# Adjacency ring of a fused graph network: zeroing only the last columns of each slot

## The chip, the core and the metric

The kernel runs on one core of a Trainium2 chip. The metric is the device time of one execution in microseconds (us), the median of several runs. Its engines are named as in the profile: PE (matrix products) with PEld (its weight loads), DVE (VectorE), ACT (ScalarE), POOL (GpSimd), SP (the queue that issues most transfers).

## What is computed

Two graph layers over 3125 nodes with 128 features and 53125 edges (25000 random pairs in both directions and one loop per node), sorted by target node `dst`. Each layer is followed by a residual and a layer norm.

```python
def _L0_gnn_ref(h, src, dst, etype, norm, weight, w_comp, bias_param):
    hsrc = h[src]
    coef = w_comp[etype]
    msg = jnp.zeros((hsrc.shape[0], weight.shape[2]), dtype=h.dtype)
    for b in range(weight.shape[0]):                       # 8 bases
        msg = msg + hsrc @ weight[b] * coef[:, b][:, None]
    msg = msg * norm
    node_repr = jax.ops.segment_sum(msg, dst, num_segments=h.shape[0])
    return jax.nn.relu(node_repr + bias_param)

def _L1_gnn_ref(node_feat, edge_feat, src, dst, eps, W1, b1, gamma, beta, W2, b2):
    msg = node_feat[src] + edge_feat
    neigh = jax.ops.segment_sum(msg, dst, num_segments=node_feat.shape[0])
    rst = (1.0 + eps[0]) * node_feat + neigh
    h = rst @ W1 + b1
    h = (h - jnp.mean(h, 0)) * jax.lax.rsqrt(jnp.var(h, 0) + 1e-5) * gamma + beta
    return jax.nn.relu(h) @ W2 + b2

x = _layernorm(x + _L0_gnn_ref(x, src, dst, edge_type_32, edge_weight1, ...))
x = _layernorm(x + _L1_gnn_ref(x, edge_attr_128, src, dst, ...))
```

## The kernel before

**Tiles, units, pairs.** The 53125 edges are 416 tiles of 128. Two tiles are a *unit* (208 units, `U`), two units a *couple* (the step `w` of DVE), four units a group, eight units a *pair* of groups (26 pairs, `PAIRS`; `PU` = 8). Since edges are sorted by target, the targets of a unit lie within a window of 20 nodes (`WIN`), and those of a pair within 132 (`SPAN`).

**First layer.** For each tile POOL gathers the 128 source rows of `x` (L719) into a ring of 32 tiles. PE multiplies them with selection matrices that DVE builds (L1302, L1312), for the 8 bases (L1004) and for the edge features of the second layer (L1010), into PSUM. DVE adds the window to `sums` (L1514). When enough units are in, a chunk of 512 nodes goes through the bases (L1034), the residual and the norm (L1042, L1406 to L1423, L1049), with ACT for the relu, the deviation and a copy (L815, L821, L826).

**Second layer, by counts.** The sum over neighbours is taken as a product with an adjacency matrix of counts. For each unit DVE makes one-hot keys of the source nodes, six units ahead (`keys_hot`, L1390 and L1393). PE turns them into counts, 25 blocks of 128 source nodes (`HIGHS`) by 20 target columns (L1025), in one of three PSUM banks. ACT copies these into the slot of the pair in SBUF, `adj_ring`, which has two slots: 25 blocks of 144 columns (`SPREAD`), float16. Unit 0 of a pair is copied to columns 0 to 19 (L805). Each later unit begins in a column that the unit ahead may also have filled, so its first column goes aside (`side`, L807) and is added by DVE (`shared_column`, L1484), and its other 19 are copied over what is there (L809), to where a register says. After the 8 units SP stores the slot to HBM (`store_adjacency`, L569), as soon as DVE has added the last shared column. Later SP loads blocks of two pairs again (L601), PE multiplies them with the first layer's result (L1058, which reads columns 0 to 131), and DVE adds the windows (L1468).

**Zeroing.** Columns that no unit of a pair copies must be zero. Before, ACT zeroes the whole slot, 3600 elements per partition in 8 pieces of 450 (`zero_adjacency`, L783). For pair 0 this comes ahead of everything; for pair p+1 it comes in two pieces behind each of the copies of units 4 to 7 of pair p, and ahead of the first of them ACT waits (`adj_out`) until the store of pair p-1, which used the same slot, has landed. DVE, PE and SP don't know of the zeroing; ACT itself waits for it ahead of unit 0 of a pair (`adj_zeroed`).

**Order of the work.** Every engine runs one list written out at build time. PE does the sums of unit u, then the counts of one or two units (`counted`: five units of counts for four of sums, so counts run ahead), and at set steps bases, transposes or a run of L1058 products. Counts of unit u wait until unit u-3 is copied. The sums of a couple wait until DVE has added the couple three back. DVE does per couple: the windows, keys, a block of L1468, the shared columns of the units that PE has counted some steps ahead, parts of the norm, and selection matrices. ACT copies in order of units, with L815, L821 and L826 between.

**The checks.** Whether all this holds for the input (windows, spans) is found early on one partition: DVE writes how far each limit is exceeded into `excess`, takes the maximum (L1347) and sets a flag (L1348). If it is above 0, all engines take a general and much slower path (`wide`).

## Time and profile before

| | |
|---|---|
| time, median of 3 runs (lowest to highest) | 769.2 us (765.85 to 769.76) |
| span of the profiled execution | 663.5 us (no time of its own is given) |
| busy: PE, PEld, DVE | 542.1, 454.7, 494.3 us |
| busy: ACT, POOL | 294.7, 415.9 us |
| mean granted TensorE clock | 0.869 |
| transfers | 108.22 MB, mean 163 GB/s |

The profile is of one execution. Its span reaches from the first to the last instruction; the time of a run has some 106 us more around it. A line of a group reads: source line, engine, operation, output <- inputs, how many, busy us and mean ns of one. In a timeline, the bracket at the end holds how long the engine was idle ahead of the instruction, and what it then waited for. "issue" is a wait for nothing that the profile shows. The granted clock is a share of 2.4 GHz. L numbers are lines of the kernel before; in the changed kernel the copies L805, L807 and L809 are L807, L809 and L811, and the zeroing L783 is L786.

### The profile page before, as it was taken

What the parts mean: (1) busy time and instruction counts of PE and PEld (TensorE: products, weight loads), DVE (VectorE), ACT (ScalarE), POOL (GpSimd) and SP (SyncE); (2) the same over time, 40 slices, a digit from 0 to 9 for tenths busy, and PEclk for the clock granted to TensorE, in tenths of its full rate; (3) what the DMA queues carried; (4) which work ended last, traced back from release to release, by engine and by line L of the source; (5) the groups of instructions that cost most, each with busy time, mean ns of one, the idle gap of its engine ahead of it and who ended that gap; (6) DMA issues with size and microseconds to landing.
All of it is one profiled execution on the core that took longest, in us unless ns stands there. A gap on an engine that the chain in (4) does not pass through costs nothing.

```text
span 663.5 us, 13490 instructions
## 1 busy us (share of the span) xinstructions
PE 542.1 (82%) x3971; PEld 454.7 (69%) x3971; DVE 494.3 (74%) x1866; ACT 294.7 (44%) x672; POOL 415.9 (63%) x434
## 2 busy tenths in 40 slices
PE   4777778887767797887789688798689999999893
PEld 3567767856757566765568577677579789868573
DVE  6998879778878858888846877858886476445456
ACT  9836545555664545644435545345440000000274
POOL 6777777777777777777756676657667777200000
PEclk9969667779677787788996689898789999999998
DMA  5414556646656647568547467657659774760003
GB/s 129 119 52 114 146 164 196 190 143 175 178 154 189 182 158 188 155 189 243 170 114 212 135 197 217 216 153 223 182 161 277 230 232 149 228 259 2 2 1 97
DMA packets 97036, 108.22 MB, mean 163 GB/s; under 512 B 10805, under 2 KB 81446, under 8 KB 96962
## 3 DMA queue, kind: packets, MB, share of 16 engines
q1 hardware_dynamic: 80898, 79.25, 39.2%
q0 software_dynamic: 13312, 27.29, 15.1%
q10 hardware_dynamic: 2752, 0.79, 0.6%
q8 instruction: 34, 0.56, 0.4%
q14 instruction: 40, 0.33, 0.2%
HBM read 81.73 MB, written 25.56 MB: 162 GB/s over the span
## 4 chain that ended last, share of the span: by engine, by line
PE 39%; DVE 35%; issue 7%; DMA 7%; ACT 6%; DVEq 5%; ACTq 0%; SPq 0%
PE psum L1058 12%; PE psum L1004 8%; DVE etype_hot L1393 7%; DMA adjacency<-adj_flat 7%; DVE etype_hot L1390 6%; PE psum L1010 5%; PE psum L1034 5%; DVE sums_flat L1514 5%; PE psum L1025 4%; DVE adj_flat L1484 3%; DVE weighted L1312 3%; ACT adj_flat L783 2%; ACT adj_flat L809 2%; DVE adj_flat L1288 2%; PE psum L1188 1%
## 5 line engine op out<-in xcount | busy, mean ns | idle before, releaser
L719 POOL DMA_INDIRECT gathered_flat<-in_x_dram,src_i x416 | 413.7, 994 | 152.8 <-issue 89.0
L1004 PE MATMUL psum<-weighted,gathered_flat 128*128 128x160 f32 (+1 forms) x832 | 163.3, 326 | 4.4 <-DVE weighted L1312 2.3
L783 ACT ACTIVATE adj_flat<-zero_col 128x450 f16<-128x450 f32 x208 | 108.9, 582 | 121.2 <-DMA adjacency<-adj_flat 110.9
L1004 PEld LDWEIGHTS psum<-weighted,gathered_flat 128*128 128x128 f32 x832 | 145.9, 225 | 17.0 <-issue 14.9
L1025 PE MATMUL psum<-etype_hot 128*128 128x300 f16 (+2 forms) x624 | 110.9, 299 | 50.0 <-ACT adj_flat L809 26.0
L1514 DVE TENSOR_TENSOR sums_flat<-psum,sums_flat 128x180 f32 x208 | 71.7, 345 | 88.8 <-PE psum L1010 56.7
L1393 DVE TENSOR_SCALAR etype_hot<-iota_key,key_t 128x300 f16<-128x300 f16 (+1 forms) x416 | 134.7, 326 | 0.0
L1010 PEld LDWEIGHTS psum<-hot,attrs 128*128 128x128 f32 x832 | 127.5, 219 | 0.0
L1010 PE MATMUL psum<-hot,attrs 128*128 128x20 f32 (+1 forms) x832 | 122.9, 264 | 0.0
L1025 PEld LDWEIGHTS psum<-etype_hot 128*128 128x128 f16 x624 | 67.5, 130 | 66.1 <-issue 28.9
L809 ACT ACTIVATE adj_flat<-psum 128x475 f32 x182 | 107.5, 591 | 0.2 <-issue 0.2
L1390 DVE TENSOR_SCALAR etype_hot<-iota_key,gathered_flat 128x128 f16<-128x128 f16 x416 | 102.5, 246 | 0.1
L807 ACT ACTIVATE gathered_flat<-psum 128x25 f16<-128x25 f32 x182 | 34.8, 191 | 109.3 <-PE psum L1025 85.2
L1058 PE MATMUL psum<-sums_flat 128*128 128x264 f16 x570 | 73.0, 286 | 9.1 <-DVE sums_flat L1468 9.1
L1312 DVE TENSOR_TENSOR weighted<-hot,coef 128x640 f32<-128x640 f32 x104 | 72.7, 740 | 1.8
L1058 PEld LDWEIGHTS psum<-sums_flat 128*128 128x128 bf16 x570 | 56.6, 101 | 22.6 <-issue 12.3
L1484 DVE TENSOR_TENSOR adj_flat<-gathered_flat,adj_flat 128x25 f16 x182 | 47.8, 265 | 22.7 <-DVE adj_flat L1484 18.0
L1058 PE MATMUL psum<-coef,sums_flat 128*128 128x264 f16 x330 | 53.2, 325 | 8.1 <-DVE sums_flat L1468 8.0
L1468 DVE TENSOR_TENSOR sums_flat<-psum,sums_flat 128x132 f32 x130 | 38.1, 293 | 22.4 <-DVE sums_flat L1468 6.5
L1034 PE MATMUL psum<-sums_flat,gathered_flat 128*128 128x512 f32 (+1 forms) x112 | 51.0, 592 | 4.0 <-DVE sums_flat L1468 4.0
L1058 PEld LDWEIGHTS psum<-coef,sums_flat 128*128 128x128 bf16 x330 | 37.1, 115 | 19.9 <-issue 10.2
L815 ACT ACTIVATE sums_flat<-psum,bias_col 128x512 f32<-128x512 f32 x6 | 4.1, 686 | 64.3 <-PE psum L1034 64.3
(144 smaller groups left out, 356.2 us busy)
## 6 DMA issues: line engine op xcount, KB each, us to landing
attrs<-in_edge_attr_dram SPq DMA_DIRECT2D x51, 512.0 KB
adjacency<-adj_flat SPq DMA_DIRECT2D x26, 900.0 KB, 4.9
sums_flat<-adjacency SPq DMA_DIRECT2D x13, 576.0 KB, 8.8
gathered_flat<-in_x_dram,src_i POOLq DMA_INDIRECT x416
coef<-adjacency SPq DMA_DIRECT2D x23, 288.0 KB, 7.1
sums_flat<-adjacency SPq DMA_DIRECT2D x5, 648.0 KB, 8.6
sums_flat<-adjacency SPq DMA_DIRECT2D x9, 288.0 KB, 5.9
out_dram<-gathered_flat SPq DMA_DIRECT2D x6, 256.0 KB
```

Source lines behind the costliest of these rows:

```text
L719: pool.indirect_dma_start(gathered[:, t % (RING * GROUP), :], None, x[:, :], bass.IndirectOffsetOnAxis(src_i[:, t:t + 1], 0)).then_inc(gat ...
L783: piece = nc.scalar.activation(adj_ring[:, s, j * size:(j + 1) * size], zero_col[:, 0:1].to_broadcast([P, size]), ACT.Copy)
L809: nc.scalar.activation(target[:, :, bass.ds(places[u % GU] + 1, WIN - 1)], counts[:, :, 1:WIN], ACT.Copy).then_inc(counts_copied, 1)
L1004: nc.tensor.matmul(ps[:, 0:B, STARTS[i]:STARTS[i] + WIDTHS[i]], gathered[:, (u * UNIT + i) % (RING * GROUP), 0:F], weighted_tiles(s, i)[:, ...
L1010: last = nc.tensor.matmul(ps[:, B, STARTS[i]:STARTS[i] + WIDTHS[i]], attrs[:, s * GROUP + j, :], hot_tiles(s, i)[:, u % GU, :], start=(i = ...
L1025: last = nc.tensor.matmul(adj_counts(u)[:, :, lo:hi], low_hot[:, u % KEYRING, i, :], source[:, :, lo - STARTS[i]:hi - STARTS[i]], start=(i ...
L1034: product = nc.tensor.matmul(bank, w_base[:, b, :], sums[:, b, k * CHUNK:k * CHUNK + n], start=(b == 0), stop=(b == B - 1))
L1058: product = nc.tensor.matmul(psum[:, bank, 0:BLOCK * SPAN], x1_part(k, c)[:, i * F:(i + 1) * F], counts[:, :, 0:SPAN], start=(h == tiles[0 ...
L1312: last = nc.vector.tensor_tensor(weighted_tiles(s % 2, i), hot_tiles(s % 2, i).unsqueeze(2).to_broadcast([P, HALF, B, n]), coef[:, g * GRO ...
L1390: nc.vector.tensor_scalar(low_hot[:, u % KEYRING, i, :], iota_key[:, 0:P], low_t[:, t:t + 1], None, ALU.is_equal)
L1393: last = nc.vector.tensor_scalar(key_hot[:, u % KEYRING, i, 0:n], iota_key[:, 0:n], key_t[:, t:t + 1], None, ALU.is_equal)
L1514: nc.vector.tensor_tensor(window, unit_psum(u), window, ALU.add).then_inc(added, 1)
```

## The change

ACT zeroes only columns 96 to 131 of each of the 25 blocks, in one instruction per pair. It stands behind the copy of unit 7 of the pair ahead, and the wait for the store of the pair two back stands with it. For the first two pairs columns 96 to 143 are zeroed, so that the slot holds no stray values when it is stored for the first time. Columns below 96 are no longer zeroed: the copies of the eight units cover them without a gap, provided that the last unit of the pair begins at column 76 (96 - 20) or later. That is a new check with 26 numbers, one per pair.

```diff
+FILLED = 96
...
-    assert HIGHS * SPREAD % GROUP == 0
+    assert FRONT + WIN <= FILLED < SPAN <= SPREAD
...
-        ranges = (U - 1, U - 1, U, U, LOOPED, 8, PAIRS)
+        ranges = (U - 1, U - 1, U, U, LOOPED, 8, PAIRS, PAIRS)
...
-            def zero_adjacency(s, j):
-
-                size = HIGHS * SPREAD // GROUP
-                piece = nc.scalar.activation(adj_ring[:, s, j * size:(j + 1) * size],
-                                             zero_col[:, 0:1].to_broadcast([P, size]), ACT.Copy)
-                if j == GROUP - 1:
-                    piece.then_inc(adj_zeroed, 1)
+            def zero_tail(p):
+
+                if p >= 2:
+                    act.wait_ge(adj_out[p % 2], 16 * (p // 2))
+                end = SPREAD if p < 2 else SPAN
+                nc.scalar.activation(pair_counts(p)[:, :, FILLED:end],
+                                     zero_col[:, 0:1].unsqueeze(2).to_broadcast([P, HIGHS, end - FILLED]),
+                                     ACT.Copy).then_inc(adj_zeroed, 1)
...
-                for j in range(GROUP):
-                    zero_adjacency(0, j)
+                zero_tail(0)
                 for u in range(U):
                     for c in range(counted(u - 1), counted(u)):
-                        p, j = c // PU, c % PU
                         copy_counts(c)
-                        if p + 1 < PAIRS and j >= PU // 2:
-                            if j == PU // 2 and p >= 1:
-                                act.wait_ge(adj_out[(p + 1) % 2], 16 * ((p + 1) // 2))
-                            for i in range(2):
-                                zero_adjacency((p + 1) % 2, 2 * j - PU + i)
+                        if c % PU == PU - 1 and c // PU + 1 < PAIRS:
+                            zero_tail(c // PU + 1)
...
+            nc.vector.tensor_scalar(excess[7], in_pairs(behind)[:, :, PAIR - 1, GU - 1], -1.0, float(FILLED - WIN),
+                                    ALU.mult, ALU.add)
```

How this moves ACT's instructions, in the second half of pair 1, from the copy of its unit 4 on. A copy of one unit is the three rows L807, ISA, L809 (`gathered_flat` is where `side` lies). Before:

```order
L807 ACTIVATE gathered_flat<-psum 128x25 [waits counts_mm,counts_added,counts_copied]
L809 ISA
L809 ACTIVATE adj_flat<-psum 128x25x19
L783 ACTIVATE adj_flat<-zero_col 128x450 [waits adj_out0]
L783 ACTIVATE adj_flat<-zero_col 128x450
L807 ACTIVATE gathered_flat<-psum 128x25 [waits counts_mm,counts_added,counts_copied]
L809 ISA
L809 ACTIVATE adj_flat<-psum 128x25x19
L783 ACTIVATE adj_flat<-zero_col 128x450 x2
```

After the change, the same pair, from the copy of its unit 7 on:

```order
L809 ACTIVATE gathered_flat<-psum 128x25 [waits counts_mm,counts_added,counts_copied]
L811 ISA
L811 ACTIVATE adj_flat<-psum 128x25x19
L786 ACTIVATE adj_flat<-zero_col 128x25x36 [waits adj_out0]
L794 TENSOR_LOAD base_row
L807 ACTIVATE adj_flat<-psum 128x25x20 [waits counts_mm,adj_zeroed]
L809 ACTIVATE gathered_flat<-psum 128x25 [waits counts_mm,counts_added,counts_copied]
```

The wait for the store (`adj_out0`) has moved from behind unit 4 to behind unit 7, and what directly follows it is the copy of unit 0 of the next pair.

On DVE, in the checks ahead of the main loop, there is one row more, L1342. Before:

```order
L1341 SCALAR_TENSOR_TENSOR coef<-psum,coef 1x26 [waits prep]
L1343 TENSOR_SCALAR coef<-base_row 1x208
L1344 TENSOR_SCALAR coef<-base_row 1x208
L1346 COPY coef<-psum 1x8 [waits turned]
L1347 TENSOR_REDUCE extremes<-coef 1x1 [waits prep]
```

After:

```order
L1338 SCALAR_TENSOR_TENSOR coef<-psum,coef 1x26 [waits prep]
L1340 TENSOR_SCALAR coef<-base_row 1x208
L1341 TENSOR_SCALAR coef<-base_row 1x208
L1342 TENSOR_SCALAR coef<-base_row 1x26
L1345 COPY coef<-psum 1x8 [waits turned]
L1346 TENSOR_REDUCE extremes<-coef 1x1 [waits prep]
```

It stands in line with the others, and the flag for which all engines wait comes behind it. PE, POOL and SP have the same instructions in the same order.

## Rows read from the trace of the kernel before

**Rows 1.** The page: busy us by engine, and the chain that ended last, by engine.
```profile
PE 542.1 (82%) x3971; PEld 454.7 (69%) x3971; DVE 494.3 (74%) x1866; ACT 294.7 (44%) x672; POOL 415.9 (63%) x434
...
PE 39%; DVE 35%; issue 7%; DMA 7%; ACT 6%; DVEq 5%; ACTq 0%; SPq 0%
```
**Rows 2.** Waits of ACT, 42 to 500 us: us in total, times, longest.
```profile
ACT adj_flat L783 <- DMA adjacency<-adj_flat: 110.9, 24, 8.6
```
**Rows 3.** Timeline: start us, us, what; first copy, then end of pair 2.
```profile
45.60 0.59 ACT L805 ACTIVATE adj_flat<-psum 128x500 f16<-128x500 f32 x1 [1.52 <-PE psum L1025]
...
81.93 0.34 SPq L569 DMA_DIRECT2D adjacency<-adj_flat  x1
...
82.64 0.66 PE L1004 MATMUL psum<-weighted,gathered_flat 128*128 128x160 f32 x4
...
83.83 0.66 PE L1004 MATMUL psum<-weighted,gathered_flat 128*128 128x160 f32 x4
...
87.13 1.04 ACT L783 ACTIVATE adj_flat<-zero_col 128x450 f16<-128x450 f32 x2 [4.72 <-DMA adjacency<-adj_flat]
...
88.85 0.74 PE L1025 MATMUL psum<-etype_hot 128*128 128x300 f16 x3 [3.67 <-ACT adj_flat L809]
...
92.42 1.19 PE L1004 MATMUL psum<-weighted,gathered_flat 128*128 128x160 f32 x4
```
**Rows 4.** Waits of PE, 42 to 500 us.
```profile
PE psum L1025 <- ACT adj_flat L809: 26.0, 14, 4.3
PE psum L1025 <- DVE etype_hot L1393: 23.7, 13, 3.9
...
PE psum L1042 <- ACT sums_flat L815: 4.8, 2, 2.6
```
**Rows 5.** Waits of DVE, 42 to 500 us.
```profile
DVE sums_flat L1514 <- PE psum L1010: 33.5, 19, 7.9
```
**Rows 6.** The gathers (L719), whole span: ns min/median/max, first and last start.
```profile
L719 POOL DMA_INDIRECT gathered_flat<-in_x_dram,src_i x416: 938/944/1569, 6.0 to 568.9; - x139
...
  issue: 89.0, 292
  PE psum L1004: 53.0, 98
```
**Rows 7.** Busy us by stage: stretch, length, PE, PEld, DVE, ACT, POOL, PEclk, DMA, GB/s.
```profile
42.00:130.00 88.00, 72.58 (x453) 67.03 (x454) 73.07 (x309) 49.55 (x129) 67.49 (x68) 0.70 0.52 150
130.00:500.00 370.00, 296.73 (x2022) 247.37 (x2022) 293.26 (x1175) 185.23 (x477) 265.04 (x267) 0.85 0.62 180
500.00:578.00 78.00, 76.75 (x633) 68.59 (x634) 45.08 (x132) 2.28 (x5) 53.67 (x54) 1.00 0.70 214
```
**Rows 8.** Groups of ACT, whole span: busy us, mean ns of one.
```profile
L783 ACT ACTIVATE adj_flat<-zero_col 128x450 f16<-128x450 f32 x208 | 108.9, 582 | 121.2 <-DMA adjacency<-adj_flat 110.9 <-DVE coef L1293 10.3
...
L757 ACT ACTIVATE sums_flat<-zero_col 128x12576 f32<-128x12576 f32 x1 | 10.7, 10667 | 0.0
```
**Rows 9.** Waits of DVE, 60 to 130 us, then 130 to 300 us.
```profile
DVE sums_flat L1514 <- PE psum L1010: 5.6, 6, 1.7
...
DVE sums_flat L1514 <- PE psum L1010: 9.4, 5, 4.3
```
**Rows 10.** Timeline: single waits of DVE and PE.
```profile
237.79 0.83 DVE L1514 TENSOR_TENSOR sums_flat<-psum,sums_flat 128x180 f32 x2 [4.34 <-PE psum L1010]
...
349.04 0.66 PE L1042 MATMUL psum<-ident,sums_flat 128*128 128x128 f32 x4 [2.65 <-ACT sums_flat L815]
...
351.11 0.83 DVE L1514 TENSOR_TENSOR sums_flat<-psum,sums_flat 128x180 f32 x2 [2.77 <-PE psum L1010]
...
435.11 0.83 DVE L1514 TENSOR_TENSOR sums_flat<-psum,sums_flat 128x180 f32 x2 [3.02 <-PE psum L1010]
```
**Rows 11.** Timeline: one of the checks on DVE.
```profile
17.39 0.18 DVE L1341 SCALAR_TENSOR_TENSOR coef<-psum,coef 1x26 f32<-1x26 f32 x1
```
**Rows 12.** The chain in order of time: where the tail begins.
```profile
578.26 8.59 PE psum L1034 x32
```

## The prediction

> **What bounds the kernel now.** I read the page first, then the waits, then single instructions around one pair boundary, then a table by stage. The page: ScalarE (ACT) is busy for 294.7 us of 663.5, so work taken off it is worth nothing by itself [rows 1]. The chain that ended last gives 7%, some 45 us, to transfers, although a store should lie beside other work. The waits say where it enters: ACT stands 110.9 us, in 24 places, until a store has landed, always ahead of a zeroing piece (L783) [rows 2]. That is the wait which the change moves.
>
> One boundary shows how it reaches the others [rows 3]. ACT has copied unit 4 of pair 2 and stands. The store of pair 1 is issued at 81.93, and ACT goes on at 87.13, after 4.72 us idle. It zeroes two pieces and copies unit 5, and only then PE's next count products start (88.85, 3.67 us idle, until ACT L809). They belong to unit 0 of the next pair, for a bank of counts is free for unit u when unit u-3 has been copied. Behind a stall PE is also slow: the same four L1004 products take 0.66 us at 83.83 and 1.19 us at 92.42, the two levels of the clock.
>
> How much of that is on the path? PE waits 26.0 us for ACT's copies between 42 and 500 us, plus 4.8 us for ACT L815, which is queued behind the same stall [rows 4]. But VectorE (DVE) is nearly full: it is idle for PE only 33.5 us of these 458 [rows 5]. GpSimd (POOL) is fuller still: 416 gathers of 944 ns (median) with 89.0 / 292 = 0.30 us between two of them; beyond that 0.30 it waits for PE only 53.0 - 98 x 0.30 = 23.6 us [rows 6]. So three engines run at nearly one pace, and what PE wins counts only as far as DVE and POOL had to wait for it.
>
> From 500 us on nothing of this acts: PE is busy 76.75 of 78 us at clock 1.00 [rows 7], and from 578 us follows the tail, which the change doesn't touch. Both shift as a whole.
>
> **The change, part by part.**
>
> *ACT's work.* 208 pieces of 582 ns go (121 us; 108.9 by the page, which takes off overlaps). The new piece has 25 x 36 = 900 elements. From 582 ns for 450 and 10667 ns for 12576 elements one element costs (10667 - 582) / 12126 = 0.83 ns [rows 8], so 582 + 450 x 0.83 = 957 ns. 26 of these (two with 1200 elements, 1.21 us) make 25.4 us. ACT sheds some 84 us. Counted at nothing: its cover is ACT's own idle time. Should the gaps between its runs of 36 cost something, two of the old pieces, 1164 ns for the same 900 elements, are the upper end, and 582 ns, one of them, the lower; neither changes the sum.
>
> *Ahead of the first copy* now one piece of 1.21 us in place of eight. The first copy, at 45.60, follows 1.52 us in which ACT waited for PE's counts [rows 3]: ACT was early already, no gain. Without that cover it would be 8 x 0.58 - 1.21 = 3.5 us.
>
> *The wait.* It stood behind the copy of unit 4, it now stands behind that of unit 7. Queued behind it on ACT: before, the copies 5 to 7 and the next pair's first; now that first copy alone, with one piece of 0.96 us in front where two stood (1.04 us). What used to hold PE at unit 8 (copy 5 late) can hold it at unit 11 (copy 8 late). Three units of sums and counts lie between: PE does one in 1.19 us at the high clock (82.64 to 83.83), and by the ratio 1.19/0.66 of the same products in about 2.15 at the low one [rows 3], so 3.6 to 6.4 us for three. PE's 14 stalls for ACT have a mean of 1.9 us and a longest of 4.3 [rows 4]. Above 3.6 us there can be seven at most (26.0/3.6); with four of them, at 4.0, 4 x 0.4 = 1.6 us are left. The store's issue hangs on DVE's shared columns, not on ACT, and no queue's order moves: SP, POOL and PE have the same rows.
>
> *What is late next.* With the stall gone PE waits for DVE's keys (23.7 us today) or DVE for PE's sums. I take DVE as the measure, since a microsecond in which it idles for PE is one the loop loses, and count its waits that have the stall behind them [rows 9, 10]: 60 to 130 us, 5.6; 130 to 300 us, 9.4 less the 4.34 at 237.79 (there PE's base products had themselves waited for DVE), 5.1; 300 to 500 us, only the 2.77 at 351.11, where PE's L1042 had waited 2.65 us for ACT (349.04), and the 3.02 at 435.11, also behind a wait of PE for ACT, 5.8. The rest of the 33.5 us, the longest of 7.9 among them, belongs to runs of products and stays. Sum 16.5 us.
>
> *The check.* One DVE instruction on 26 numbers, 0.18 us as L1341 with its 26 numbers; the reduction over all checks grows by 3%. 0.2 us, and as I can't show that DVE has a gap there, it counts [rows 11].
>
> *Sum*: 16.5 - 1.6 - 0.2 = 14.7 us. The span goes from 663.5 to 648.8, and the time, as much lies outside the span as before, from the median 769.2 to **754.5**. The page gives no time of its own for the profiled execution; the three runs lie between 765.85 and 769.76, so a change under 0.5%, 3.8 us, can't be told from none.
>
> Bounds of this term: at the low end nothing, if DVE merely swaps these idle times for others; at the high end POOL's 23.6 us and a few more, since the last gather starts at 568.9 and PE enters the tail at 578.26 [rows 6, 12], 9.4 us later, where one gather and the sums of a unit, some 4, would do: 29 us.
>
> **The rivals.**
>
> *POOL becomes the bound.* If the clock stays high without the 4 us stalls, PE needs half the time per unit and catches up with the gathers. For it: the clock is 0.70 and 0.85 where stalls stand and 1.00 where none do [rows 7]. Against: DVE's 33.5 us hold some 17 that have other causes, so PE would wait for DVE. Gain 18 to 29 us, say 22: 747.
>
> *The time was hidden anyway.* DVE is busy for 366 of these 458 us [rows 7] and has small gaps of its own; what it idled for PE behind a stall it may idle elsewhere, for products at the low clock or for base products. For it: of ACT's 24 waits only 14 are seen by PE, and of 110.9 us only 26.0 [rows 2, 4]. Against: the waits of DVE in the first stretch come one upon the other with the stalls. Then only that stretch yields its 5.6 us or less: gain 0 to 8, say 5: 764.
>
> *Slower, by the clock.* Now PE stands still once per pair for 4 us and may then run densely. Paced by DVE it would instead wait often and shortly. If that keeps it at the low level for longer, base products and runs of products lengthen like L1004 above (0.66 to 1.19), and they are on the path. Between 130 and 500 us PE is busy 296.7 us at a mean clock of 0.85 [rows 7]. At 0.70, as between 42 and 130 us, that would be 360, 63 more; the chain gives PE 39% of the span [rows 1], so 25 us come through, against the 14.7 gained: 780. It decides from where it costs more than 14.7, that is 38 us more busy time, a clock of 0.75. Against it: where the trace shows short waits only (500 to 578) the clock is 1.00, if with far denser work. The Trainium skill (TensorE: Matmul & The Clock Gate, A second HAM failure mode: psum-queue depth-cycling) says that frequent short idle times between groups of matmuls make the clock gate go back and forth; by that rule this case would come about, and the trace agrees only in that the clock is lowest (0.70) in the stretch with most waits.
>
> *The change doesn't take effect.* The new check needs the last unit of each pair to start at least 96 - 20 = 76 nodes behind the first. There are 53125/3125 = 17 edges per node and 256 per unit, so 15 nodes per unit and about 105 for seven. Otherwise the general path would run: 416 x 25 = 10400 rounds of several instructions, of which each costs at least the 0.18 us of the small one in [rows 11], so over 1900 us more.
>
> **How the numbers follow.** Forecast (gain 8 to 18, 751 to 761): 0.52. POOL as bound: 0.15. Hidden anyway: 0.24, half of it above 3.8 us of gain. Clock: 0.08. General path: 0.01. So faster 0.52 + 0.15 + 0.12 = 0.79, same 0.12, slower 0.09. The range 742 to 766 takes in the forecast, nearly all of POOL's case and the hidden case down to 3 us of gain; left out are the slower cases, 0.09, and some 0.08 of the hidden one.
>
> **What the changed profile would show.** ACT's zeroing x26 with about 0.96 us each, 25 us busy. ACT's wait for the store near 25 us in place of 110.9, about 1 us in most pairs and up to 4 in the pair that showed 8.6. PE's wait for ACT L809 (now L811) under 5 us, its wait for DVE's keys larger. DVE's wait for PE between 42 and 500 us near 17 in place of 33.5. POOL's last gather near 555, the start of the tail near 564. The forecast is wrong if DVE's waits for PE keep their 33 us (hidden anyway), if POOL's waits beyond 0.30 us vanish (POOL as bound), or if the clock up to 500 us falls below 0.75.

## The result, and the profile after

| | before | after |
|---|---|---|
| time, median of 20 runs (lowest to highest) | 768.12 us (762.87 to 771.14) | 762.79 us (757.96 to 769.91) |
| ratio, 95% interval | | 0.9937 (0.9918 to 0.9956) |
| profiled execution of after: time, span | | 765.73 us, 763.9 us |
| mean granted TensorE clock | | 0.813 |

The change gains 5.3 us (3.4 to 6.3 by the interval: 0.0044 to 0.0082 of 768). The forecast was 14.7. Time and span of the profiled run differ by 1.8 us. The 106 us that the prediction, and the section on the time before, took to lie around the span therefore lie somewhere else, and that is the first thing to look for. The page of after, busy us by engine, then the chain that ended last (compare [rows 1]):

```profile
PE 585.5 (77%) x3971; PEld 481.3 (63%) x3971; DVE 496.7 (65%) x1867; ACT 227.2 (30%) x490; POOL 411.4 (54%) x434
...
PE 42%; DVE 28%; another core or an unknown queue 11%; issue 10%; DVEq 4%; ACT 3%; DMA 1%; SPq 0%; ACTq 0%
```

Transfers have gone from 7% of the chain to 1%. ACT is busy 67.5 us less (294.7 to 227.2), DVE and POOL as much as before. But the span is 763.9 against 663.5, and 11% of the chain is now ended by something that the profile can't name. The zeroing pieces (L786), then the gathers (L720, compare [rows 6]), each with what their engine waited for ahead of them:

```profile
L786 ACT ACTIVATE adj_flat<-zero_col x26: 930/943/1202, 51.9 to 553.9; 128x900 f16<-128x900 f32 x24, 128x1200 f16<-128x1200 f32 x2
...
  DMA adjacency<-adj_flat: 3.0, 2
```

```profile
L720 POOL DMA_INDIRECT gathered_flat<-in_x_dram,src_i x416: 938/944/1567, 6.4 to 650.7; - x139
...
  issue: 101.7, 322
  PE psum L1001: 63.5, 50
  DVE sums_flat L1513: 36.0, 20
  remote: 25.4, 15
```

The new piece takes 943 ns, and the stall on the store is gone. A gather takes 944 ns as before, yet the last one starts at 650.7 in place of 568.9. Waits of PE, then of DVE, 42 to 500 us (compare [rows 4, 5]; L1513 and L1007 are L1514 and L1010 of before), then the stages (compare [rows 7]):

```profile
PE psum L1022 <- ACT adj_flat L811: 31.0, 18, 6.3
PE psum L1001 <- issue: 17.0, 20, 3.1
PE psum L1022 <- issue: 10.6, 11, 2.1
PE psum L1022 <- DVE etype_hot L1392: 10.4, 9, 5.4
```

```profile
DVE sums_flat L1513 <- remote: 45.9, 14, 5.2
DVE sums_flat L1513 <- PE psum L1007: 38.8, 15, 6.1
```

```profile
42.00:130.00 88.00, 63.69 (x453) 56.02 (x451) 62.21 (x236) 25.12 (x62) 56.47 (x59) 0.66 0.39 111
130.00:500.00 370.00, 280.61 (x1745) 232.31 (x1744) 261.98 (x1056) 120.49 (x304) 232.42 (x237) 0.77 0.52 157
500.00:578.00 78.00, 62.21 (x447) 51.57 (x444) 54.98 (x215) 24.13 (x63) 48.74 (x50) 0.88 0.58 177
```

PE still waits 31.0 us for ACT's copies, where the prediction expected under 5, though the store holds ACT up for 3.0 us only. What holds ACT up instead is ahead of its own copies, in the same stretch:

```profile
ACT gathered_flat L809 <- remote: 111.8, 24, 8.8
```

"remote" is a wait that a semaphore ended for which the profile finds no instruction or transfer. In the same 370 us DVE and POOL finish a tenth less, PE 14% less (DVE x1056 for x1175, POOL x237 for x267, PE x1745 for x2022); a gather has the same length, and so has DVE's L1513 (345 ns in both). So this trace can't be set beside the rows ahead of the prediction: a second thing differs between them, worth 100 us, and it isn't the change. The runs below were needed to part the two. They were taken in four sets, each on one chip and beside runs of the kernel before: on one chip (two sets) it took 666 us, on two others 767 to 768. None of them was seen at both levels. Ratios are taken within a set; where they differ a little from what the medians give, the text says which of the two it uses.

### The profile page after: what moved, and what is told of

It reads as the page before. It is cut to its first block, busy times and chain, and to the rows that moved or that the text cites. A ratio compares the mean times of both kernels' runs of the same rounds, so it can differ in the third digit from the quotient of the medians.

```text
span 763.9 us, 13309 instructions
## 1 busy us (share of the span) xinstructions
PE 585.5 (77%) x3971; PEld 481.3 (63%) x3971; DVE 496.7 (65%) x1867; ACT 227.2 (30%) x490; POOL 411.4 (54%) x434
## 3 DMA queue, kind: packets, MB, share of 16 engines
q0 software_dynamic: 13312, 27.29, 12.5%
## 4 chain that ended last, share of the span: by engine, by line
PE 42%; DVE 28%; another core or an unknown queue 11%; issue 10%; DVEq 4%; ACT 3%; DMA 1%; SPq 0%; ACTq 0%
PE psum L1055 13%; PE psum L1001 8%; PE psum L1007 6%; DVE etype_hot L1392 6%; PE psum L1031 6%; PE psum L1022 5%; DVE etype_hot L1389 4%; DVE sums_flat L1513 4%; DVE adj_flat L1483 2%; DVE weighted L1309 2%; ACT adj_flat L811 2%; DVE adj_flat L1285 1%; PE psum L1185 1%; DVE sums_flat L1467 1%
## 5 line engine op out<-in xcount | busy, mean ns | idle before, releaser
L720 POOL DMA_INDIRECT gathered_flat<-in_x_dram,src_i x416 | 409.2, 984 | 239.2 <-issue 101.7
L1001 PE MATMUL psum<-weighted,gathered_flat 128*128 128x160 f32 (+1 forms) x832 | 177.5, 342 | 23.7 <-issue 20.0
L1513 DVE TENSOR_TENSOR sums_flat<-psum,sums_flat 128x180 f32 x208 | 71.8, 345 | 173.3 <-remote 75.0
L1001 PEld LDWEIGHTS psum<-weighted,gathered_flat 128*128 128x128 f32 x832 | 156.2, 238 | 39.6 <-issue 37.1
L1022 PE MATMUL psum<-etype_hot 128*128 128x300 f16 (+2 forms) x624 | 116.7, 310 | 56.2 <-ACT adj_flat L811 33.1
L1007 PEld LDWEIGHTS psum<-hot,attrs 128*128 128x128 f32 x832 | 136.7, 232 | 10.2 <-issue 10.0
L1007 PE MATMUL psum<-hot,attrs 128*128 128x20 f32 (+1 forms) x832 | 131.5, 273 | 7.7 <-issue 7.6
L809 ACT ACTIVATE gathered_flat<-psum 128x25 f16<-128x25 f32 x182 | 35.0, 192 | 318.8 <-PE psum L1022 142.7
L1055 PE MATMUL psum<-sums_flat 128*128 128x264 f16 x570 | 83.1, 307 | 14.1 <-DVE sums_flat L1467 8.4
L1055 PEld LDWEIGHTS psum<-sums_flat 128*128 128x128 bf16 x570 | 60.9, 109 | 32.1 <-issue 17.5
L1055 PE MATMUL psum<-coef,sums_flat 128*128 128x264 f16 x330 | 50.8, 315 | 16.7 <-DVE sums_flat L1467 11.6
L1031 PEld LDWEIGHTS psum<-sums_flat,gathered_flat 128*128 128x128 f32 x112 | 20.4, 208 | 27.0 <-issue 27.0
L786 ACT ACTIVATE adj_flat<-zero_col 128x900 f16<-128x900 f32 (+1 forms) x26 | 25.0, 962 | 24.9 <-DVE coef L1290 21.9
```

The lines of the kernel that those rows point to most:

```text
L720: pool.indirect_dma_start(gathered[:, t % (RING * GROUP), :], None, x[:, :], bass.IndirectOffsetOnAxis(src_i[:, t:t + 1], 0)).then_inc(gat ...
L1001: nc.tensor.matmul(ps[:, 0:B, STARTS[i]:STARTS[i] + WIDTHS[i]], gathered[:, (u * UNIT + i) % (RING * GROUP), 0:F], weighted_tiles(s, i)[:, ...
L1007: last = nc.tensor.matmul(ps[:, B, STARTS[i]:STARTS[i] + WIDTHS[i]], attrs[:, s * GROUP + j, :], hot_tiles(s, i)[:, u % GU, :], start=(i = ...
L1022: last = nc.tensor.matmul(adj_counts(u)[:, :, lo:hi], low_hot[:, u % KEYRING, i, :], source[:, :, lo - STARTS[i]:hi - STARTS[i]], start=(i ...
L1031: product = nc.tensor.matmul(bank, w_base[:, b, :], sums[:, b, k * CHUNK:k * CHUNK + n], start=(b == 0), stop=(b == B - 1))
L1055: product = nc.tensor.matmul(psum[:, bank, 0:BLOCK * SPAN], x1_part(k, c)[:, i * F:(i + 1) * F], counts[:, :, 0:SPAN], start=(h == tiles[0 ...
```

## The experiments

### On a chip at the level of the first profile

**The kernel before once more** (no edit).

> The kernel before, once more with a profile. Its first profile had a span of 663.5 us beside timed runs of 769.2, the changed kernel's has 763.9 beside 762.8. Theory 1 (the first profile was taken in conditions in which the timed runs don't take place, with about 100 us less of waits on every engine): the new span is 764 to 770, PE is idle much longer, and VectorE's waits in the loop are 100 us or more instead of 50. Theory 2 (the span of before is really 663, and the changed kernel has gained 100 us of waits inside and lost them outside): the span is 660 to 668 again.

Measured: 670.83 us with a span of 669.0, beside a median of 666.4 for the same kernel (11 runs). Theory 1 has its number wrong, as this chip isn't that of the timed runs; theory 2 has its number within 1 us, but not its reason, since the time falls with the span. So what was profiled first was a machine on which this kernel takes 666 us, and what was timed was one on which it takes 768. Nothing lies outside the span but 1.8 us. From here on two levels are kept apart: 666 and 768.

**The small piece at the old place.** The change's zeroing, but behind the copy of unit 4 of the pair, where the wait for the store was:

```diff
-                        if c % PU == PU - 1 and c // PU + 1 < PAIRS:
+                        if c % PU == PU // 2 and c // PU + 1 < PAIRS:
```

> The changed kernel, but with the wait and the small zeroing behind the copy of unit 4 as before, so that only the zeroing work shrinks. If the place of the wait is what gains (my theory), the time is that of before within 2 us (ratio 0.998 to 1.003). If ACT's shed work gains (rival), it is that of the changed kernel, ratio about 0.993.

**The full zeroing at the new place.** Eight pieces of 450 again, but all behind the copy of unit 7, with the wait:

```diff
-                nc.scalar.activation(pair_counts(p)[:, :, FILLED:end],
-                                     zero_col[:, 0:1].unsqueeze(2).to_broadcast([P, HIGHS, end - FILLED]),
-                                     ACT.Copy).then_inc(adj_zeroed, 1)
+                size = HIGHS * SPREAD // GROUP
+                for j in range(GROUP):
+                    piece = nc.scalar.activation(adj_ring[:, p % 2, j * size:(j + 1) * size],
+                                                 zero_col[:, 0:1].to_broadcast([P, size]), ACT.Copy)
+                piece.then_inc(adj_zeroed, 1)
```

> The changed kernel, but all 3600 elements are zeroed in 8 pieces behind the copy of unit 7, with the wait there: the wait moved, no work shed. ACT then has 4.7 us of pieces between the copy of unit 7 and that of unit 0. If the place of the wait gains, the ratio is 0.993 to 0.998; if the shed work does, it is 1.000 or above.

**The change whole** (no edit), on the same chip.

> The changed kernel on the same chip as the two parts: ratio 0.993, between 0.990 and 0.997.

Measured, all against the kernel before at 666.4 us:

| | us | ratio (95%) | ACT waits for the store | PE waits for ACT's copies | PE waits for keys |
|---|---|---|---|---|---|
| small piece, old place | 661.72 | 0.9916 (0.9883 to 0.9949) | 121.9 | 32.5 | 27.6 |
| full zeroing, new place | 657.31 | 0.9848 (0.9814 to 0.9882) | 10.0 | 6.6 | 26.5 |
| the change | 655.67 | 0.9821 (0.9786 to 0.9856) | 10.8 | not in the list | 37.3 |

Here the change gains 1.8%, 11.9 us (by the ratios; the medians differ by 10.7). Moving the wait alone gives 10.1 us of it, shedding the work alone 5.6 (by the medians 9.1 and 4.7). The sum of 15.7 is above the 11.9, by little more than the intervals allow; that both shorten the same stall would explain it. All three expectations missed in size: the change and the moved wait gain more than their ranges allowed, and the shed work, which my theory had at nothing, is worth 0.8% by itself, the rival's number, but less than half of what the change gives here. How it can be, with a wait for the store as long as before (121.9), the run of the small piece only hints at. PE's waits for ACT, whole span, of the small piece at the old place, and of the kernel before in its first run of this section:

```profile
PE psum L1022 <- ACT adj_flat L811: 32.5, 9, 6.1
```

```profile
PE psum L1025 <- ACT adj_flat L809: 36.0, 16, 5.0
```

Nine stalls instead of sixteen (14 and 16 in the two other traces of the kernel before), while their sum is not less (26.0 and 28.5 us in those). Behind the landing ACT had two pieces of 0.58 us after each of four copies, and now has one piece in all, so the copies of units 6 and 7 come some 1 and 2 us earlier, and the small stalls that follow the first one can go. This is argued: the execution that was profiled took 667.09 us, the longest of its seven, and its tail starts no earlier than before (580.06), so the trace doesn't show the gain. The time does: ACT's work behind the stall was not free.

A second set on this chip confirmed the size, with six runs of the change and 17 of the kernel before.

> The changed kernel, unchanged, as the reference of the next two runs. At a level of 768 us for the kernel before: ratio 0.990 to 0.996 as measured before on such an occasion. At 666 us: 0.979 to 0.986.

Measured: 655.14 against 666.63 us, ratio 0.9821 (0.979 to 0.9852); the medians differ by 11.5 us, the ratio gives 11.9. Its trace may now be set beside rows 1 to 12. The zeroing and its wait, the gathers, waits of PE and of DVE from 42 to 500 us:

```profile
L786 ACT ACTIVATE adj_flat<-zero_col x26: 932/943/1202, 40.4 to 472.5; 128x900 f16<-128x900 f32 x24, 128x1200 f16<-128x1200 f32 x2
...
  DMA adjacency<-adj_flat: 10.0, 8
```

```profile
L720 POOL DMA_INDIRECT gathered_flat<-in_x_dram,src_i x416: 939/947/1580, 6.1 to 557.6; - x139
```

```profile
PE psum L1022 <- DVE etype_hot L1392: 33.6, 18, 4.4
...
DVE sums_flat L1513 <- PE psum L1007: 23.3, 15, 4.9
```

The wait for ACT is no longer in PE's list, which is the step that the prediction asked for first. PE's wait for keys is up from 23.7 to 33.6 us, so some 10 of the 26 us of stall may only have changed their name. DVE's wait for PE falls by 10.2 (33.5 to 23.3), where 16.5 were forecast, and that is nearly the gain: the tail starts at 568.75 in place of 578.26. These sums vary from trace to trace: the kernel before has 33.5, 36.3 and 32.7 us, the change 22.2 and 23.3, so the fall is 9 to 14 us. The chain in order of time:

```profile
568.75 8.59 PE psum L1031 x32
```

### On chips at the level of the timed runs

**More work on DVE.** If DVE paces the loop, DVE work added to it should cost its length. One of the keys of every unit is written in two halves: 208 more instructions, DVE busy for 25.5 us more (521.6 against 496.1 us). Done to the kernel before and to the change:

```diff
-                    nc.vector.tensor_scalar(low_hot[:, u % KEYRING, i, :], iota_key[:, 0:P], low_t[:, t:t + 1],
-                                            None, ALU.is_equal)
+                    for lo, hi in ((0, P // 2), (P // 2, P)) if i == 0 else ((0, P),):
+                        nc.vector.tensor_scalar(low_hot[:, u % KEYRING, i, lo:hi], iota_key[:, lo:hi],
+                                                low_t[:, t:t + 1], None, ALU.is_equal)
```

> The kernel before, with VectorE's key of 128 elements of the first tile of each unit written in two instructions of 64 (208 instructions more, by 64 against 128 elements some 0.12 to 0.18 us each, 25 to 35 us of VectorE in all). If VectorE paces the loop, much of this appears, 12 us or more (ratio 1.018 and up); if the stall of ScalarE hides it, less than 8 us (under 1.012).

> The same addition in the changed kernel, leading to a ratio against the kernel before. My theory: without the stall VectorE paces the loop, so at least as much appears as in the kernel before, 15 us or more over the changed kernel (ratio 0.982 + 0.023 = 1.005 or above). Rival (GpSimd's gathers pace it): under 6 us over the changed kernel, ratio 0.982 to 0.991.

Measured, against 767.63 us (23 runs): 771.85, ratio 1.0056 (1.0019 to 1.0094), and 770.39, ratio 1.0031 (0.999 to 1.0073). The kernel before takes 4.2 us more, the change 7.6 more than its 762.79 of another set (both to within some 3 us). The first lies where the stall of ScalarE hides the addition, the second between its two theories. So at this level a sixth to a third of added DVE time shows. DVE is part of what sets the pace, but not the measure of it.

**Half of the gathers.** In the change, the gather of the second tile of a unit is left out from unit 16 on (192 of 416 gathers; PE multiplies old rows there).

```diff
-                for t in range(u * UNIT, (u + 1) * UNIT):
+                for t in range(u * UNIT, (u + 1) * UNIT if u < RU else u * UNIT + 1):
...
-                    pe.wait_ge(gather_in[u % RU], (u // RU + 1) * 16 * UNIT)
+                    pe.wait_ge(gather_in[u % RU], 16 * UNIT + u // RU * 16)
```

> The changed kernel without the gather of the second tile of each unit from unit 16 on (PE then multiplies old rows of that tile; left out: 192 of 416 gathers). Theory (VectorE paces): ratio 0.975 to 0.983, at most 4 us under the changed kernel. Rival (GpSimd or the transfers pace): 15 us or more under it, ratio below 0.96.

Measured: 665.37 us, ratio 0.8661 (0.8613 to 0.8709), against 767.63. The rival had the direction, but it is far more than its 15 us: this takes off nearly the whole distance between the levels, and the rest has a place: ahead of unit 16 all gathers are still there, and in this run ACT's first zeroing waits 21.9 us for DVE's coefficients, 11.4 more than the change does at the lower level.

```profile
L786 ACT ACTIVATE adj_flat<-zero_col x26: 932/943/1202, 51.8 to 480.7; 128x900 f16<-128x900 f32 x24, 128x1200 f16<-128x1200 f32 x2
...
  DVE coef L1290: 21.9, 1
```

Without these 11.4 it would be 654.0 us, the change's own time at 666 (655). POOL's busy time doesn't fill the loop: in the profiled run of the change POOL is idle for 239 us ahead of its gathers, 102 of them the 0.3 us that lie between any two.

**The kernel before at the upper level.** This and the next two ran on a third chip, with the kernel before at 766.68 us.

> The kernel before, unchanged, one profiled look. If its time is near 768 us: theory 1 (at that level PE and DVE wait mostly for something that comes with the gathers, and the stall on the store is only a part of it) expects ACT's wait for the store within 20% of 115 us and PE's wait for ACT's copies within 10 us of the 33.1 us that the changed kernel shows at this level. Theory 2 (the stall costs as much as at 666 us, and the change gives something back) expects PE's wait for ACT's copies above 50 us. If its time is near 666 us it repeats two looks and tells nothing new.

Measured: 767.88 us, span 766.1. Waits over the whole span, first at the upper level, then of the same kernel at the lower one (a run of 665.05 us, whose expectation stands at the end of this section):

```profile
ACT gathered_flat L807 <- remote: 94.7, 24, 7.8
...
ACT adj_flat L783 <- DMA adjacency<-adj_flat: 76.9, 19, 7.4
...
DVE sums_flat L1514 <- PE psum L1010: 66.9, 29, 6.2
DVE sums_flat L1514 <- remote: 66.1, 21, 10.0
...
PE psum L1025 <- issue: 32.6, 19, 6.0
...
PE psum L1025 <- DVE etype_hot L1393: 22.8, 13, 4.8
...
PE psum L1025 <- ACT adj_flat L809: 17.6, 13, 4.6
```

```profile
ACT adj_flat L783 <- DMA adjacency<-adj_flat: 113.2, 24, 9.1
...
DVE sums_flat L1514 <- PE psum L1010: 55.9, 31, 7.9
...
PE psum L1025 <- ACT adj_flat L809: 28.5, 16, 4.5
...
PE psum L1025 <- DVE etype_hot L1393: 22.3, 14, 3.9
```

Both theories missed with their numbers (76.9 against 92 to 138, 17.6 against 23 to 43), the second by far more (over 50). What they show is that the stall itself is smaller here: ACT stands 76.9 us for 113.2, a third less (in the one other trace of the old zeroing at this level with all gathers, that with DVE's added work, 91.8). (Why isn't shown; this trace has no landing times of the stores. If other waits make ACT come later to this one, it would be so.) And a new kind of wait has come up, "remote": 94.7 us for ACT's L807 and 66.1 us for DVE's L1514, where the nine traces at the lower level list none at all, on any engine. The timeline of this run from 94.8 to 102.2 us shows what it looks like (the bracket: idle us ahead, and for what):

```profile
94.85 1.33 PE L1025 MATMUL psum<-etype_hot 128*128 128x300 f16 x6
...
95.98 0.85 PE L1004 MATMUL psum<-weighted,gathered_flat 128*128 128x160 f32 x4
...
96.67 0.52 PE L1010 MATMUL psum<-hot,attrs 128*128 128x20 f32 x4
...
97.32 0.94 POOL L719 DMA_INDIRECT gathered_flat<-in_x_dram,src_i  x1 [0.31 <-issue]
99.44 0.19 ACT L807 ACTIVATE gathered_flat<-psum 128x25 f16<-128x25 f32 x1 [4.75 <-remote]
...
100.27 0.74 PE L1025 MATMUL psum<-etype_hot 128*128 128x300 f16 x3 [3.07 <-ACT adj_flat L809]
100.31 0.83 DVE L1514 TENSOR_TENSOR sums_flat<-psum,sums_flat 128x180 f32 x2 [5.54 <-remote]
```

PE has done its counts at 96.2 and its sums at 97.2. ACT waits for these counts and DVE for these sums, and the trace shows nothing else ahead of them; yet ACT starts at 99.44 and DVE at 100.31. Between 98.26, the end of the gather, and 99.44 no engine does anything. Added up from the traces (instructions of the sequencers counted as work), all four of PE, DVE, ACT and POOL stand at once for 19.0 us between the first and the last gather of this run, for 21.8 us in the profiled run of the change, and for 11 to 26 us in the other three of this level with all gathers. At the lower level it is 0.2 to 0.8 us in eight traces, and in no single place over 0.05.

**Indirect, or just a transfer?** In the change, the second tile of a unit is fetched by a plain transfer on POOL's queue, of 128 neighbouring rows that are not those of the edges; as many bytes and as many landings.

```diff
+                    if u >= RU and t % UNIT:
+                        pool.dma_start(gathered[:, t % (RING * GROUP), :],
+                                       x[7 * u:7 * u + P, :]).then_inc(gather_in[u % RU], 16)
+                        continue
```

> The changed kernel with the second tile of every unit from unit 16 on fetched by a plain transfer of 128 neighbouring rows on POOL's queue, in place of a gather of 128 rows by index: as many bytes and rows, the rows are not those of the edges. At a level of 768 us: if the indirect addressing makes the 100 us, about 665 us (ratio 0.86 to 0.88) as without these gathers; if bytes and landings make them, 0.98 to 1.00. At 666 us: 0.975 to 0.99, as the changed kernel.

Measured: 665.73 us, ratio 0.8654 (0.8583 to 0.8724), the same as without these transfers at all. So it isn't bytes or landings, nor the number of packets (13312 packets and 27.29 MB on this queue, as with all gathers). It is the indirect form of these transfers, or what comes with it, that goes with the 100 us: POOL takes 944 ns for each, and the 128 rows lie scattered in memory. Neighbouring rows fetched by index, or scattered ones without, were not tried, so form and scatter are not told apart. All four engines stand at once for 1.6 us in this run.

**The kernel before with half of its gathers.** The same omission as above, on the kernel before.

> The kernel before with the second tile's gather left out of every unit from unit 16 on (192 of 416 gathers left out, PE multiplies old rows there). At a level of 768 us: theory 1 (the gathers' cost covers the gain, and without it the gain comes back) expects it 9 to 14 us above the 665 us of the changed kernel with the same omission, ratio 0.878 to 0.885; theory 2 expects it within 6 us, 0.862 to 0.874. At 666 us: 0.993 to 0.998 as measured before.

Measured: 676.35 us, ratio 0.8821 (0.877 to 0.8871), against 0.8661 and 0.8654 for the change with fewer indirect gathers. That is 10.6 us above the latter, on the same chip (four runs each, of 674 to 678 and 661 to 671 us): the size that the change has at 666 us, as the first theory said. The trace has the picture of the lower level again: ACT waits 115.1 us for the store, and "remote" is down to 9.6 us in three places, the longest of 6.3 us at L1293, ahead of the loop.

```profile
ACT adj_flat L783 <- DMA adjacency<-adj_flat: 115.1, 24, 8.9
```

The same kernel at the lower level:

> The kernel before with the second tile's gather left out of every unit from unit 16 on, as in the run of the changed kernel with half of its gathers. Left out: 192 of 416 gathers, PE multiplies old rows there. Theory 1 (the gathers' cost at this level covers the gain of the change, and without it the gain comes back in full): at a level of 768 us for the kernel before, this one is 9 to 14 us above the 665 us of that run, ratio 0.878 to 0.885. Theory 2 (the gain is small at this level for another reason): within 6 us of it, ratio 0.862 to 0.874. At a level of 666 us: POOL as the bound of the kernel before expects a gain of over 10 us (ratio under 0.985), DVE as its measure expects a ratio of 0.99 to 1.00.

Measured: 664.47 us, ratio 0.9957 (0.9929 to 0.9985). Halving POOL's work in the loop (busy 124.45 us between 130 and 500 us in place of 266.48) is worth 0.4%, which speaks for DVE as the measure there, and against POOL. From it to the 676.35 of the same kernel at the upper level it is 11.9 us, again the wait ahead of the loop. So the 100 us go with indirect gathers on two of the three chips, and with nothing in the change.

The run of the kernel before whose trace serves as the lower level above; at 665.05 us it decides nothing between its theories:

> The kernel before, unchanged, one profiled look on this occasion, so that its waits can be set beside those of the changed kernel at the same level of time. If its time is near 768 us: theory 1 (at that level PE and DVE wait mostly for something that comes with the gathers, and the stall on the store is only a part of it) expects ACT's wait for the store within 20% of the 115 us of the level at 666, PE's wait for ACT at L809 within 10 us of the 33.1 us that the changed kernel shows at this level, and DVE's waits for PE (L1514) within 10 us of the changed kernel's. Theory 2 (the same stall as at 666 us, and something else given back by the change) expects PE's wait for ACT at L809 above 50 us. If its time is near 666 us this run tells nothing new.

### A version that goes on from there

If PE's wait for keys is what the gain ran into, keys that come earlier should be worth something. On DVE's list the shared columns of three or four units (0.27 us each, most with a small wait ahead) stand behind all keys of a couple; now one of them stands behind each unit's keys, ahead of the next unit's, as long as there are any.

```diff
-                    for c in range(min(U, counted(2 * w - 2) + KEYRING), min(U, counted(2 * w) + KEYRING)):
+                    added_now = [c for c in ripe if c % PU]
+                    fresh = list(range(min(U, counted(2 * w - 2) + KEYRING), min(U, counted(2 * w) + KEYRING)))
+                    for c in fresh:
...
+                        if added_now:
+                            s = added_now.pop(0)
+                            shared_column(s, shares[s // GU][s % GU])
...
-                    for c in ripe:
-                        if c % PU:
-                            shared_column(c, shares[c // GU][c % GU])
+                    for c in added_now:
+                        shared_column(c, shares[c // GU][c % GU])
```

> The changed kernel, with VectorE's shared columns placed between the keys of units instead of behind them, in order to fill the 0.23 us that each waits for the one ahead (18.7 us in 79 places in the changed kernel). Theory (VectorE paces): 4 to 14 us under the changed kernel, ratio 0.962 to 0.976. Rival (these gaps lie beside other waits): within 3 us of the changed kernel, ratio 0.978 to 0.987.

> The changed kernel with DVE's shared columns placed between the keys instead of behind them. Theory 1 (PE's wait for keys is what the gain runs into next, and a key that comes about 1 us earlier is worth something): ratio to the kernel before 0.003 to 0.010 under that of the unchanged changed kernel in this call. Theory 2 (the order on DVE is worth nothing, since DVE has the same work either way): within 0.002 of it.

Measured at the upper level: 758.71 us, ratio 0.9891 (0.9839 to 0.9942), which overlaps the change's 0.9937, so there it can't be told from the change (the 4.1 us between the medians touch the low end of the theory and lie just outside the rival's 3). At the lower: 646.11 us, ratio 0.9679 (0.9643 to 0.9714), where the change has 0.9821 in the same set: 9.0 us more by the medians, beyond what either theory allowed for the size. One of its six executions took 1190.81 us; nothing here explains it. Without it the median is 645.22, and the ratio leaves it out. Of this version, waits over the whole span at 666:

```profile
POOL gathered_flat L720 <- PE psum L1001: 24.4, 80, 0.3
PE psum L1001 <- DMA gathered_flat<-in_x_dram,src_i: 24.1, 12, 5.0
...
PE psum L1022 <- DVE etype_hot L1392: 19.3, 13, 2.7
```

PE's wait for keys has gone from 33.6 to 19.3 us. But two things changed at once: DVE's small waits ahead of its shared columns, each for the one before, have gone too, from 20.0 us in 84 places to 0.7 in 3. Which of the two gives the 9.0 us is not told apart. POOL never waits more than 0.3 us for PE, and PE now waits 24.1 us for gathers, a wait that PE's list shows in none of the other traces. DVE waits longer for PE than before, 47.6 us between 42 and 500 us in place of 23.3, and yet the loop is shorter. This is what the first rival of the prediction, POOL as the bound, would show, arriving one change later; and it shows that DVE's wait for PE measures the loop only while DVE is what paces it. This version beats both kernels at the lower level, and the kernel before at the upper one.

## Why the prediction was wrong, point by point

**The step that failed: "the time, as much lies outside the span as before".** The difference of 106 us between the median and the span was taken to be something around the span, constant, to which the sum of a 663.5 us trace could be added. Only 1.8 us lie around it. The other 104 are two chips: the profile was taken where the kernel takes 666 us, the times where it takes 768, as far as the spans tell. Of the 102.8 us between the spans of the kernel before in its second and third run here, 11.6 lie ahead of the loop (ACT's first zeroing waits 10.4 us for DVE's coefficients at one level and 22.0 at the other), 91.2 in the loop, and nothing in the tail, which takes 85.3 us from its start in both (663.3 - 578.03, 766.1 - 680.84). So the rows were right, but of a chip on which the stalls of the loop are others, and the sum was carried over to one where the stall on the store is smaller and much of what it frees is taken up by waits of another kind. There the path that the prediction freed, PE behind ACT's copies, isn't freed at all: PE waits for them for 17.6 us before and 33.1 after (whole span, one trace each), while ACT's wait for the store falls from 76.9 to 3.0 and its "remote" wait ahead of L807, now L809, grows from 94.7 to 122.3. A profiled span over 13% under every timed run was the sign, and it should have counted as a doubt about every term, with a case and a chance of its own.

**The sum at its own level: right in kind, too high in size.** 14.7 us were forecast, 11.9 measured by the ratio in both sets (10.7 and 11.5 by the medians), and the forecast lies just beyond the high end of both intervals (0.9786 and 0.979 are 14.3 and 14.0 us). The term that was mis-sized is "16.5", DVE's waits that have the stall behind them: between the first trace and the last of the change, DVE's waits for PE from 42 to 500 us fell by 10.2. By stretch, 60 to 130 us gave 4.1 (5.6 to 1.5; 5.6 forecast), 130 to 300 us nothing (9.4 to 9.8), where 5.1 were to go, and 300 to 500 us 6.4 (17.1 to 10.7; 5.8 forecast). The last agrees by luck. Of the two waits picked there, the 2.77 us at 351.11 went, but the 3.02 at 435.11 is still there, while 5.7 us came from the wait that was to stay, because it "belongs to runs of products". The first two lines are of the kernel before: PE's wait for keys, and DVE's 7.88 us some 10 us later. The two after them are of the change, and no other wait of DVE for PE there is above 1.3 us from 300 us on:

```profile
328.78 0.49 PE L1025 MATMUL psum<-etype_hot 128*128 128x300 f16 x3 [3.87 <-DVE etype_hot L1393]
...
339.26 0.82 DVE L1514 TENSOR_TENSOR sums_flat<-psum,sums_flat 128x180 f32 x2 [7.88 <-PE psum L1010]
```

```profile
330.09 0.35 DVE L1513 TENSOR_TENSOR sums_flat<-psum,sums_flat 128x180 f32 x1 [2.22 <-PE psum L1007]
...
425.70 0.83 DVE L1513 TENSOR_TENSOR sums_flat<-psum,sums_flat 128x180 f32 x2 [3.53 <-PE psum L1007]
```

The 7.9 us stand in all three traces of the kernel before (7.8 to 7.9), and in that of the small piece at the old place (7.8); in both traces of the change they are 2.1 and 2.2, and 2.2 where only the wait was moved. In the kernel before, PE waits 3.87 us for keys ahead of the same run of products, a wait that the change's trace doesn't have there. So the sum over waits is about right, but not wait by wait: those picked out because a stall precedes them needn't go with it, and one that stands behind a run of products can go. PE's wait for keys over the whole loop grew by 10, which was named as what is late next, but no price was put on it.

**"Left over stalls, 1.6".** At the lower level none is left that PE's list shows. ACT's own wait fell to 10.0 us in place of the 25 named, and PE never saw it. The bound by three units of lead held with room.

**"ACT's work: counted at nothing".** Alone it is worth 0.8% (0.5 to 1.2). The cover named, ACT's idle time, is no cover for pieces that lie behind the stall, where PE is waiting for ACT. The price of the new piece, 957 ns, was right (943; its own working gives 956).

**"The check, 0.2".** Too small to be seen in any run.

**The rivals.** *Hidden anyway* had 764 us as its number and lies nearest the 762.79 measured. At the lower level its mechanism isn't what happened: there DVE's waits for PE did fall, by 10 us. At the upper level it describes the outline, if not the reason it gave: DVE's waits ahead of L1514 from 42 to 500 us, for PE and "remote" together, are 77.8 us before and 84.7 after (L1513), one trace each, so what is freed in one place is idle in another, in waits that the rows couldn't show. *POOL as the bound*: not at the lower level, where half of the gathers left out are worth 0.4% to the kernel before. *Slower by the clock*: at the lower level the mean granted clock between 130 and 500 us stays at 0.84 to 0.85 with the change, and the many short waits for keys that this case needs are there (18, in place of 13). The 0.77 of the change at the upper level is also that of the kernel before there:

```profile
130.00:500.00 370.00, 277.55 (x1732) 231.25 (x1733) 261.58 (x1056) 168.29 (x431) 233.61 (x235) 0.77 0.53 156
```

The Trainium skill (TensorE: Matmul & The Clock Gate, A second HAM failure mode: psum-queue depth-cycling) would have the clock go back and forth with such waits. The traces at the lower level don't bear out the rule for this kernel. Between the kernel before and the change, with 13 and 18 waits for keys, the clock has not moved; and the interleaved version, where PE waits 13 times for keys and 12 times for gathers, has 0.89 in this stretch, more than either (part of it because its last run of products begins ahead of 500 us). The prediction's own sign, the clock of 0.70 "in the stretch with most waits", is a weak one: PE has 10 waits of over 0.2 us in those 88 us and 37 in the 370 after them, nearly as many per us. *The change doesn't take effect*: no, the trace of the change shows its pieces and copies (x26), and no general path.

**What stays open.** Why an indirect gather costs so much on two of the chips. The runs show that it does, that PE's results then reach ACT and DVE some 3 us late in the place shown, with gathers around it, that plain transfers of neighbouring rows in place of half of them end it, and that the gathers themselves last as long as ever (944 and 947 ns). Whether the late signal is that of the waiting instruction's semaphore or of something ahead of it, the traces don't show. Nor is it shown whether a level belongs to the chip or to something that stood around it in these sets, as no chip was seen at both. Nor how much of the missing 6 us at that level went to the smaller stall and how much to such waits: the runs with half of the gathers take away both at once.

## What to carry to other kernels

Set a profile's span beside the timed runs first: if they differ by more than a run has around its span (1.8 us here), they come from two situations, and a sum made from one is no forecast for the other until a trace of the second is at hand. Work on an engine that is mostly idle isn't free when it stands between a late landing and the result that the next engine waits for; look at which side of the stall the idle time lies. And where three engines run at nearly one pace, a stall taken away is paid out only as far as the next wait allows: put a price on that wait, or move what feeds it (here the order of keys and shared columns, worth 9.0 us once the stall was gone). A sum over waits that comes out right can be made of single waits that don't: check it wait by wait before trusting the rule that picked them.

## What the runs showed of the hardware

- The same program takes 666 us on one chip and 767 to 768 on two others, with instructions of the same length (gather 944 and 947 ns, DVE's L1514 345 and 344 ns). With 192 of 416 indirect gathers left out, or made plain transfers of neighbouring rows, the upper level is 665 to 676 us.
- At the upper level ACT and DVE start some 3 us after the PE results (in the place shown) that they wait for, and all four engines stand at once for 11 to 26 us of a run (0.2 to 0.8 us on the other chip).
- On POOL issuing a plain transfer of 128 rows takes 603 ns, an indirect gather of as many 976 in the same run (min/median/max ns):

```profile
L724 POOL DMA_INDIRECT gathered_flat<-in_x_dram,src_i x224: 943/976/1561, 6.3 to 553.7; - x112
L721 POOL DMA_DIRECT2D gathered_flat<-in_x_dram x192: 571/603/781, 56.3 to 554.7; - x192
```

- On ACT, 900 elements in 25 runs of 36 take 943 ns, where 582 ns for 450 in one run and 0.83 ns for each further element give 956: the gaps between runs cost nothing that shows.
